# The four-bit feed-forward stage of a layer program: a power of two made on ScalarE, gate times up on VectorE, and other lags

## The reference, cut to what matters

```python
def fp4_quant_dequant(x):               # blocks of 16 along the last dim
    xb = x.reshape(shape[:-1] + (shape[-1] // BLOCK, BLOCK))
    scale = jnp.max(jnp.abs(xb), axis=-1, keepdims=True) / 6.0
    scale = jnp.maximum(scale, jnp.float32(1e-12))
    xn = xb / scale
    idx = jnp.searchsorted(_MID, jnp.abs(xn))       # 0.25 0.75 1.25 1.75 2.5 3.5 5
    q = _GRID[idx] * jnp.sign(xn) * scale           # 0 0.5 1 1.5 2 3 4 6
...
gate = fp4_linear(x, w_gate)            # x: normalised rows, 256; gate, y: 704
y = fp4_linear(x, w_up)
h = jax.nn.silu(gate) * y
return fp4_linear(h, w_down)            # h quantised too, back to 256
```

## Time and profile before

| | us |
|---|---|
| median of 3 runs | 2827.17 |
| lowest, highest run | 2812.53, 2828.0 |
| profiled execution, span from first to last instruction | 2816.7 |
| TensorE busy | 2497.9 (89%) |
| VectorE busy | 2077.3 (74%) |
| ScalarE busy | 1248.8 (44%) |
| GpSimd busy | 865.1 (31%) |

### The profile page before, as it was taken

One profiled execution on the slowest core, in us unless ns is written; L12 is line 12 of the kernel. 1 busy time (PEld: TensorE's weight loads), 2 busy tenths in 40 slices (PEclk: granted clock), 3 DMA queues, 4 the chain that ended last, 5 costly groups with the idle time before them and its releaser, 6 DMA issues. The chain is left out here.

```text
span 2816.7 us, 44565 instructions
## 1 busy us (share of the span) xinstructions
PE 2497.9 (89%) x16076; PEld 2270.6 (81%) x16076; DVE 2077.3 (74%) x3623; ACT 1248.8 (44%) x1992; POOL 865.1 (31%) x517
## 2 busy tenths in 40 slices
PE   7999996788888886999999999994988889699999
PEld 6888885778877885889888988883887778599998
DVE  5666666999999996655665566547899998766664
ACT  4444443444434432544554565432433334344444
POOL 1111112656665652320232023204334433211110
PEclk9999997998999997999999999976999999899999
DMA  5000000000000000000000000002000010000000
GB/s 162 0 0 0 0 0 18 1 1 0 0 0 0 0 1 15 1 15 15 7 7 15 11 7 11 15 12 68 16 23 15 15 45 0 32 24 23 22 22 30
DMA packets 43119, 45.99 MB, mean 16 GB/s; under 512 B 2977, under 2 KB 42017, under 8 KB 42785
## 3 DMA queue, kind: packets, MB, share of 16 engines
q1 hardware_dynamic: 43040, 44.95, 5.0%
HBM read 28.16 MB, written 16.78 MB: 16 GB/s over the span
## 5 line engine op out<-in xcount | busy, mean ns | idle before, releaser
L1745 ACT ACTIVATE m_a<-m_ps_wide,m_b 128x512 f32<-128x512 f32 x128 | 88.3, 690 | 286.4 <-PE m_ps_wide L277 201.1
L1713 PE MATMUL m_ps_z<-m_w_hi,m_a_hi 128*128 128x256 f32 x512 | 152.7, 298 | 52.8 <-DVE m_a_lo L1785 52.8
L275 PE MATMUL f_ps_down<-f_down_w_hi,f_h_T_hi 128*128 128x256 f32 (+1 forms) x384 | 132.9, 346 | 68.1 <-DVE f_h_T_lo L932 68.1
L1745 ACT ACTIVATE d_a<-d_ps_wide,d_b 128x512 f32<-128x512 f32 x128 | 88.3, 690 | 190.5 <-PE d_ps_wide L277 190.4
L1785 DVE TENSOR_TENSOR d_a_lo<-d_a,d_a_hi 128x512 fp32r<-128x512 f32 x128 | 86.7, 689 | 111.8 <-ACT d_a_hi L1749 111.4
L1237 POOL TENSOR_TENSOR p_kf<-p_kf,p_k_shift 128x1024 f32<-128x1024 f32 x64 | 119.4, 1902 | 155.5 <-DVE p_k_shift L1371 155.5
L1713 PEld LDWEIGHTS m_ps_z<-m_w_hi,m_a_hi 128*128 128x128 f32 x512 | 103.2, 202 | 67.0 <-DVE m_a_lo L1785 62.0
L187 ACT ACTIVATE f_h_magic<-f_h_magic,minus_magic 128x1408 f32<-128x1408 f32 x32 | 47.1, 1473 | 240.7 <-DVE f_h_magic L183 240.7
L275 PEld LDWEIGHTS f_ps_down<-f_down_w_hi,f_h_T_hi 128*128 128x128 f32 (+1 forms) x384 | 84.8, 221 | 84.3 <-DVE f_h_T_lo L932 74.2
L1713 PE MATMUL m_ps_z<-m_w_lo,m_a_hi 128*128 128x256 f32 x512 | 149.9, 293 | 0.0
L1713 PE MATMUL m_ps_z<-m_w_hi,m_a_lo 128*128 128x256 f32 x512 | 149.8, 293 | 0.0
(11 more groups left out here) (342 smaller groups left out, 9081.5 us busy)
## 6 DMA issues: line engine op xcount, KB each, us to landing
residual<-in_x SPq DMA_DIRECT2D x8, 1024.0 KB, 11.8
attn<-p_attn SPq DMA_DIRECT2D x32, 256.0 KB, 2.1
m_attn<-attn SPq DMA_DIRECT2D x16, 512.0 KB, 3.9
out<-residual SPq DMA_DIRECT2D x16, 512.0 KB, 2.9
raw_weights<-in_d_q SPq DMA_DIRECT2D x2, 1024.0 KB, 7.2
d_scale<-in_d_scale SPq DMA_DIRECT2D x2, 1024.0 KB, 5.9
raw_weights<-in_m_w1T SPq DMA_DIRECT2D x1, 1024.0 KB, 5.1
raw_weights<-in_m_w2T SPq DMA_DIRECT2D x1, 1024.0 KB, 9.7
```

The source lines that it names most:

```text
L275: pe.matmul(out, lhsT[0], rhs[0], start=start, stop=False)
L1713: mm = pe.matmul(z, a, w[:, f, :], start=(f == 0 and k == 0 and j % 2 == 0), stop=(f == FC - 1 and k == 2), skip_group_check=True)
L1745: act.activation(self.a[f % RING][:, :], self.ps_wide[f % 2][:, :], self.func, bias=self.b1[:, f:f + 1])
```

## The change

- The exponent passes on VectorE go, for weights, n and h. ScalarE makes |v| times 2^22 in one pass straight from v, written in the rounded fp32r format, and the two rounding passes on VectorE take the greater of that and 1.5 x 2^22 in place of a sum.
- ScalarE no longer copies up; VectorE multiplies silu by up straight out of PSUM, in two steps of 704 columns per tile, and GpSimd no longer multiplies.
- The lists of all four engines get other lags (greatest 8) and another order.
- The last half chunk of h: the turned chunk takes the last 128 columns of h, high and low part are stacked in one chunk of 128 rows, with the down weights laid out to match, so that two matmuls take the place of three; ScalarE's two copies become one. The weights' preparation gets a memset and a copy at its end, with waits.

```diff
-    def exponents(self, dve, v):
-        return dve.tensor_scalar(self.magic[:, :].bitcast(I32), v.bitcast(I32), EXPONENT, None, ALU.bitwise_and)
-    def steps(self, act):
-        return act.activation(self.magic[:, :], self.magic[:, :], ACT.Relu, scale=MAGIC, bias=self.core.minus_magic[:, :])
+    def steps(self, act, v):
+        return act.activation(self.magic[:, :], v, ACT.Abs, scale=LIFT)
     def round(self, dve, step, v):
-        m = self.magic[:, :]
-        step.add(dve.scalar_tensor_tensor(v, m, MAGIC, v, ALU.add, ALU.add))
+        m = self.magic[:, :].bitcast(F32)
+        step.add(dve.scalar_tensor_tensor(v, m, MAGIC, v, ALU.max, ALU.add))
         step.wait()
-        return dve.scalar_tensor_tensor(v, m, MAGIC, v, ALU.add, ALU.subtract)
+        return dve.scalar_tensor_tensor(v, m, MAGIC, v, ALU.max, ALU.subtract)
...
+                dve.wait_ge(w_lo, len(fills))
+                dve.memset(down_w[1][0:FL, KF - 1, :].bitcast(F32), 0.0).then_inc(w_lo, 1)
+                dve.tensor_copy(down_w[0][0:FL, KF - 1, :], ps_w[(len(fills) - 1) % 4][FL:P, 0:D]).then_inc(w_lo, 1)
+                dve.wait_ge(w_lo, len(fills) + 2)
...
-            pipeline(pool, N, [(6, multiply), (2, divide_n), (3, restore_n), (6, divide_h), (7, restore_h)], SLOTS)
+            pipeline(pool, N, [(6, divide_h), (6, restore_h), (3, restore_n), (2, divide_n)], SLOTS)
...
+            def multiply(j):
+                def phase(t, s):
+                    dve.wait_ge(silu_ready, G * t + j + 1)
+                    dve.wait_ge(up_done, G * t + j + 1)
+                    wait_count(dve, h_turned, G * (t - SLOTS + 1))
+                    dve.tensor_tensor(h_q[s][:, j * FF:(j + 1) * FF].rearrange("p (a n) -> p a n", a=2), ps_up[:, :, 0:FH],
+                                      silu[:, j, :].rearrange("p (a n) -> p a n", a=2), ALU.mult).then_inc(h_ready, 1)
+                return phase
...
-                    dve.tensor_tensor(lo[0:FL, full:KF * P], ps_h[0:FL, full:KF * P],
-                                      hi[0:FL, full:KF * P].bitcast(F32), ALU.subtract).then_inc(h_lo, 1)
+                    dve.tensor_tensor(hi[0:FL, full:KF * P], ps_h[FL:P, full:KF * P], hi[FL:P, full:KF * P].bitcast(F32),
+                                      ALU.subtract).then_inc(h_lo, 1)
-            pipeline(dve, N, [(7, exponents_h), (3, exponents_n), (9, add_down), (4, split_n), (3, round_n), (8, split_h(0)), (6, scales_h), (7, round_h), (8, split_h(1)), (1, scales_n)], SLOTS)
+            pipeline(dve, N, [(8, add_down), (4, split_n), (7, split_h(0)), (3, round_n), (6, round_h), (5, multiply(0)),
+                              (7, split_h(1)), (2, scales_n), (5, multiply(1)), (5, scales_h)], SLOTS)
...
-                    act.wait_ge(up_done, G * t + j + 1)
-                    act.activation(up[:, j, :].rearrange("p (a n) -> p a n", a=2), ps_up[:, :, 0:FH],
-                                   ACT.Copy).then_inc(up_ready, 1)
...
-                    act.activation(hi[:, 0:full], ps_h[:, 0:full], ACT.Copy).then_inc(h_hi, 1)
-                    act.activation(hi[0:FL, full:KF * P], ps_h[0:FL, full:KF * P], ACT.Copy).then_inc(h_hi, 1)
+                    act.activation(h_T[j][0][:, :], ps_h[:, 0:KF * P], ACT.Copy).then_inc(h_hi, 1)
...
-            pipeline(act, N, [(7, steps_h), (4, high_n), (3, steps_n), (8, high_h(0)), (1, normalise), (5, gate(0)), (8, high_h(1)), (5, gate(1))], SLOTS)
+            pipeline(act, N, [(4, high_n), (7, high_h(0)), (3, steps_n), (6, steps_h), (5, gate(0)), (7, high_h(1)),
+                              (1, normalise), (5, gate(1))], SLOTS)
...
-                w, ps, done, read = ((gate_w, ps_gate, gate_done, silu_ready), (up_w, ps_up, up_done, up_ready))[which]
+                w, ps, done, read = ((gate_w, ps_gate, gate_done, silu_ready), (up_w, ps_up, up_done, h_ready))[which]
...
+                    last = h_T[j][0][:, (KF - 1) * P:KF * P]
+                    pe.matmul(out, last, down_w[0][:, KF - 1, :], start=False, stop=False)
+                    mm = pe.matmul(out, last, down_w[1][:, KF - 1, :], start=False, stop=True)
...
-            pipeline(pe, N, [(4, turn_n), (8, turn_h(0)), (5, widen(0, 0)), (5, widen(0, 1)), (8, turn_h(1)),
-                             (5, widen(1, 0)), (5, widen(1, 1)), (8, narrow(0)), (8, narrow(1))], SLOTS)
+            pipeline(pe, N, [(4, turn_n), (7, turn_h(0)), (5, widen(0, 0)), (5, widen(0, 1)), (7, turn_h(1)),
+                             (5, widen(1, 0)), (7, narrow(0)), (5, widen(1, 1)), (7, narrow(1))], SLOTS)
```

More of the change, by code:

```diff
@@ L36 @@
 G = 2
-EXPONENT = 0x7F800000
-MAGIC = 1.5 * 2.0 ** 22
+LIFT = 2.0 ** 22
+MAGIC = 1.5 * LIFT
 TIE = 1.0 + 2.0 ** -22
@@ L210, in __init__ @@
         self.loaded, self.cleared = core.sem("f_raw_loaded"), core.sem("f_raw_cleared")
-        self.step, self.scaled, self.divided, self.masked, self.stepped, self.rounded, self.quantised = (
-            core.sem(f"f_w_{e}") for e in ("step", "scaled", "divided", "masked", "stepped", "rounded", "quantised"))
+        self.step, self.scaled, self.divided, self.stepped, self.rounded, self.quantised = (
+            core.sem(f"f_w_{e}") for e in ("step", "scaled", "divided", "stepped", "rounded", "quantised"))
     def allocate(self):
@@ L241, in vector @@
             dve.sem_inc(self.scaled, 1)
-        elif stage == 1:
-            dve.wait_ge(self.divided, b + 1)
-            self.fp4.exponents(dve, self.piece(b)).then_inc(self.masked, 1)
-        else:
+        elif stage == 2:
             dve.wait_ge(self.stepped, b + 1)
@@ L250, in scalar @@
     def scalar(self, act, b):
-        act.wait_ge(self.masked, b + 1)
-        self.fp4.steps(act).then_inc(self.stepped, 1)
+        act.wait_ge(self.divided, b + 1)
+        self.fp4.steps(act, self.piece(b)).then_inc(self.stepped, 1)
     def divide(self, pool, b):
@@ L770, in fp4_layer @@
                         fills.append((moves, P, c1 - c0, part(w, slice(None), c, slice(c0, c1))))
-            for r in range(KF):
-                rows = min(P, FF - r * P)
-                moves = [(weights.down[:, c, r * P:r * P + rows], c * P) for c in range(D // P)]
-                fills.append((moves, rows, D, part(down_w, slice(0, rows), r)))
+            for r in range(KF - 1):
+                moves = [(weights.down[:, c, r * P:(r + 1) * P], c * P) for c in range(D // P)]
+                fills.append((moves, P, D, part(down_w, slice(None), r)))
+            moves = [(weights.down[:, c, FF - P:FF], c * P) for c in range(D // P)]
+            fills.append((moves, P, D, part(down_w, slice(None), KF - 1)))
             block = prep.enter_context(nc.Block())
@@ L792, in _ @@
                     for src, at in moves:
-                        mm = pe.transpose(ps_w[n % 4][0:src.shape[1], at:at + src.shape[0]], src,
+                        mm = pe.transpose(ps_w[n % 4][0:rows, at:at + src.shape[0]], src,
                                           ident[0:src.shape[0], 0:src.shape[0]])
@@ L961, in phase @@
                     wait_count(act, down_done, G * (t - 1) + j + 1)
-                    hi, full = h_T[j][0], (KF - 1) * P
-                    act.activation(hi[:, 0:full], ps_h[:, 0:full], ACT.Copy).then_inc(h_hi, 1)
-                    act.activation(hi[0:FL, full:KF * P], ps_h[0:FL, full:KF * P], ACT.Copy).then_inc(h_hi, 1)
+                    act.activation(h_T[j][0][:, :], ps_h[:, 0:KF * P], ACT.Copy).then_inc(h_hi, 1)
                 return phase
             def steps_n(t, s):
-                act.wait_ge(n_masked, t + 1)
-                n_fp4.steps(act).then_inc(n_stepped, 1)
+                act.wait_ge(n_divided, t + 1)
+                wait_count(act, n_rounded, t)
+                n_fp4.steps(act, n_q[s][:, :]).then_inc(n_stepped, 1)
             def steps_h(t, s):
-                act.wait_ge(h_masked, t + 1)
-                h_fp4.steps(act).then_inc(h_stepped, 1)
+                act.wait_ge(h_divided, t + 1)
+                wait_count(act, h_rounded, t)
+                h_fp4.steps(act, h_q[s][:, :]).then_inc(h_stepped, 1)
             def normalise(t, s):
@@ L1016, in phase @@
                     for c in range(KF):
-                        rows = P if c < KF - 1 else FL
-                        at = j * FF + c * P
-                        mm = pe.transpose(ps_h[0:rows, c * P:(c + 1) * P], h_q[s][:, at:at + rows], ident[:, :])
+                        at = j * FF + min(c * P, FF - P)
+                        mm = pe.transpose(ps_h[:, c * P:(c + 1) * P], h_q[s][:, at:at + P], ident[:, :])
                     mm.then_inc(h_turned, 1)
@@ L1027, in phase @@
                     pe.wait_ge(h_lo, 2 * (G * t + j + 1))
-                    for c in range(KF):
-                        rows = P if c < KF - 1 else FL
-                        mm = product(pe, ps_down[:, j * D:(j + 1) * D], part(h_T[j], slice(0, rows), slice(c * P, (c + 1) * P)),
-                                     part(down_w, slice(0, rows), c), start=(c == 0), stop=(c == KF - 1))
```

(11 more changed lines are left out.)

34 lines of the change are left out of this document (8 added, 26 removed).

## The result

The changed kernel takes 2714.09 us, median of four runs (2711.94 to 2729.2), beside 2820.18 us for the kernel before in the same session: ratio 0.9644, 95% interval 0.9608 to 0.9679. A second session gave 0.9677 (0.9629 to 0.9724). The profiled span is 2710.9 us, 105.8 us less than before. The forecast was 2712 us.

The account below looks back on a forecast made before the run. VectorE, busy 95.48 of 100 us, bounds the kernel. Turns -98, tail -6, head -10, preparation +1, attention -2: -115 us from the 2816.7 us span gives 2702, plus 10 carried over, 2712 us; range 2685 to 2768.

Parts of the forecast that it names:

- the walk: One turn of the four-bit stage followed item by item across the engines: scales of h done at 14.78 us.
- The 4.06 us pass: VectorE's first rounding of h: 1.60 us of work behind most of GpSimd's 2.60 us division; to become 1.6 us.
- A turn of 14.8 us: Four-bit stage, add to add: 14.8 us instead of 18.87, -98 us over 24 turns.
- The closed loop through the gate: Division, step pass, gate, second gate product, down product, second up product, multiplication 1, scales of h: sets 14.8 us a turn.
- Head -10: Ahead of the first add: 1.2 partly filled turns fewer, -10 us, between 0 and 17.8; preparation adds 1 separately.
- attention -2: Attention stage: eight weight pieces lose their exponent pass on ScalarE, -2 us, between 0 and 11.
- tail -6: From the 25th to the last add: 95.9 us against 101.4, -6 us.
- the 10 us that the prediction carried over: Whole run: the earlier median stood 10.5 us above the profiled span; 10 us added to the forecast span of 2702.
- tables are not swapped: Rival on ScalarE: new function in another table than the gate's, two swaps a turn, 16.1 us a turn, 2751 us; chance 0.05.
- the collision did not stay: Rival on VectorE: first rounding pass of h stays at 4.06 us behind GpSimd, 2771 us; chance 0.04.
- The clock's rival: TensorE's granted clock falls for 3 us a turn, lengthening it by 1.3 us, +39, 2751 us; chance 0.18.
- The slower rival: TensorE at its lower clock for most of each turn, behind the wait for the gate, up to 3010 us; chance 0.05.

Follow-up runs that it names:

- the run with the spare pass: Changed kernel plus an unused GpSimd squaring of a 128x1408 tile between dividing and restoring h each turn: turn 17.78 us, ratio 0.9851.
- GpSimd's new order: Changed kernel with GpSimd dividing n before restoring n, its list alone changed: turn 14.92 us, ratio 0.9594.
- gate first: Changed kernel with ScalarE taking the first gate before the step pass of h: turn 15.72 us, ratio 0.9654.
- both moves together: Changed kernel with VectorE's scales of n before the rounding of n and ScalarE's first gate before the step pass: turn 16.36 us, ratio 0.9708.

## Why the prediction was right, and which step was not

- *VectorE bounds the kernel, and a turn can be walked item by item:* right. With the one wait gone that the walk had missed, the turn is 14.75 us where the loop doesn't come round; the walk gave 14.78. That it is so close is in part luck: the second up product ends 0.12 us earlier than walked (0.09 of it from the step pass), and a hole of about 0.3 us that the walk didn't have stands before multiplication 1.
- *The 4.06 us pass is a collision with GpSimd, and the new order ends it:* right, shown three ways: 1.62 us after the change, 4.05 us with the old lags and the new arithmetic, and the rounding of n raised from 0.69 to 2.62 us by a pass that nobody needs. The prediction's row for PSUM readers, the split at 751.56 us, lies inside the GpSimd pass for only 0.40 of its 0.68 us; the run with the spare pass has whole splits inside one. The Trainium skill (SBUF — State Buffer, SBUF: two separate sides) says that VectorE and GpSimd share an exclusive lock, held for a whole instruction, and that VectorE takes part with two SBUF inputs or in a two-port mode. The trace agrees: PSUM readers kept 0.68 and 0.81 us beside GpSimd, and line 172, which has one input, stood as well; its mode no row shows.
- *Multiplications at 0.89 us each, exponent passes away, one table load:* right to 0.01 us. The step pass was taken at 1.47 us and is 1.38. That is what the prediction's sentence on a dropped pointer operand gave by the Trainium skill (ScalarE: Activation LUTs, What ACT_TABLE_LOAD costs); the trace agrees with the page.
- *A turn of 14.8 us:* wrong, 15.83. The failed step is "scales of n from 9.25. Their small passes wait until GpSimd's restoring ends at 10.26". The walk had the pass in the queue 0.3 us ahead of that end. In fact it came 0.05 us behind it (708.18 against 708.13), and stood behind the next pass as well: 0.82 us a turn, shown by GpSimd's new order. The fallen clock is 0.1 us a turn more, and what is left at 14.92 us is the loop, next but one below. Of the 0.34 us by which the small pass missed its place, 0.24 are the stacked chunk in the second split, which the prediction had put at "nothing on the path, bound 0.2 us either way"; the unstacked run, where line 172 is ahead again, shows it. The other 0.1 us is the shorter step pass, which let GpSimd restore earlier.
- *The closed loop through the gate decides:* right only in the walk. In the changed kernel it had 0.9 us of slack (gate first: 0.1 us). TensorE's idle 0.75 us before the second gate product is there (0.96, 1.30, and 0.80 with 0.99 more just ahead of it, in the three turns of a pass through the loop); it cost nothing but in the six turns in which the clock fell behind it.
- *Where the hardware loop comes round:* missing from the sum. One turn lasts 15.57 us, one 15.84 (the one with the fallen clock) and the third 16.26; the hole before the next turn's first item is 0.27, 0.35 and 0.77 us. Before, all 24 turns lasted 18.85 to 18.91 us.
- *Head -10, attention -2, tail -6:* -15.7 and 1 us more of preparation in it, -3.7, -3.9. The head was taken 6.7 us too low (-16.7 without the preparation), within its bound of -17.8.
- *The whole:* 2712 against 2714 us is luck, as far as it is nearer than its parts. The turns gave 25 us less than forecast and the tail 2; head and attention gave 8 more, and 9.5 us came from the unchanged rest. That makes a span of 2710.9 us where 2702 was forecast. What hid these 9 us is the 10 us that the prediction carried over as surroundings of the span: in every run on record the time is only 1.6 to 1.8 us above the span, and the rest of the 10 was the spread between runs. A fourth run of the kernel before, 2813.18 us, brought its median from 2827.17 to 2820.18.
- *Rivals:* tables are not swapped, the collision did not stay. The clock's rival was half right: a stretch of 3.4 us at the lower level (687.15 to 690.5) does come, but only in six of 24 turns, and most of it fell into the slack, so that it cost 0.1 us a turn in the mean and not 1.3. The prediction's argument against it, a dense stretch at 1.00, held for the other turns. The slower rival had its place wrong: slow turns of 22 us at a clock of 0.84 do exist, but behind multiplication 0, and only with the old lags.

## What to carry to other kernels

Where two engines block each other by whole instructions, an item that arrives a twentieth of a microsecond late pays for the other's next pass in full; give the other engine an item that must wait at that place, as dividing n first does, rather than moving the late one. When a step that frees a buffer moves to a fuller engine, walk the producer's list too: two multiplications with one product between them need 3.3 us of other work between them, whatever the engine's sum says. And look for the clock behind each longer wait of TensorE: with both moves together, what the wait cost afterwards was the whole loss. Last, judge an edit of a hundredth by the length of a turn in the trace, if the rest of the program spreads by as much.
